# A two-layer graph transformer: the first norm ahead of the edge work, degrees in two halves, transposes in mid-chunk

## The chip, the cores and the metric

The kernel runs on one core of a Trainium2 chip. The metric is the device time of one execution in microseconds (us). The kernel before took 2141.93 us, the median of three runs (2136.43 to 2147.46 us).

## The reference, cut to what matters

There are 1250 nodes of 768 features and 20000 edges, sorted by destination. `src` and `dst` are lists of 20000 int32.

```python
xn = layernorm(x)
x = x + graph_attention(xn, src, dst) + linear_attention(xn)      # elu(q)+1, elu(k)+1, 12 heads
x = x + moe0(layernorm(x))                                        # 8 experts, top 2, one matrix each
xn = layernorm(x)
x = x + gcn_2_layers(xn, src, dst) + mix1(xn)                     # w_qkv, L2 norms over the nodes
x = x + moe1(layernorm(x))                                        # 8 experts, top 2, two matrices, gelu
# gcn: deg = segment_sum(ones, dst); dinv = rsqrt(deg); norm = dinv[src] * dinv[dst]
```

Everything is float32 in and out. The edges enter as a dense count matrix of 1250 x 1250, built on the chip from the two lists; the degrees are its sums (with one self loop for each node), and are used only in the second layer's GCN.

## The kernel before, in words

The nodes are cut into ten tiles of 125 rows (`NT`, `T`); X holds all of them in SBUF, XT holds the normalised rows transposed (six blocks of 128 features by 1250 nodes). Each engine has its own program, an instruction stream that runs in order, and the streams meet only at semaphores. TensorE's results go to eight PSUM banks in rotation: `plan_jobs` (L72) lists the jobs in order, job m uses bank m modulo 8, and `begin(m)` (L579) waits until the job eight places before has been emptied by the engine that owns it (`act` or `dve`). The consumer waits with `full(m)` for the count of filled jobs.

**Start.** SyncE (SP) issues the loads in this order (L412 to L463): the two edge lists EI, the first group of X (tiles 0 and 1), three small loads for the attention vectors (`wide`, `attn_sb`), the value weights of the first attention (`load(1)`), X's second group (tiles 2 to 5), its third (tiles 6 to 9), a bias, four small router loads (RWS, RBI), and WBD. ScalarE (ACT) issues the key weights first of all (L1055) on a queue of its own. VectorE (DVE) sets constants, then waits for the edge lists and does the edge work (L1324 to L1391): it casts the lists (EF), and in turns with TensorE (four jobs: `edges`, `spans`, `rng`, `attn_vec`) finds for each destination tile which edge tiles touch it, writes the table of turns, and places the attention vectors in vz. Only then come the first norms: `spread_of` (statistics), a square root by ACT (`root`), `normal` (writes XN).

**Key and value loop.** For each tile t, TensorE transposes tile t+1 (`transpose_tile`, L587) and multiplies tile t by the key and the value weights (`rows`, L605 through L645 and L646: 4 jobs of 6 matmuls, each of two passes in the profile). ACT copies the transposes to XT (`turned_tile`), takes the exponential of the keys and copies the values; DVE, which in iteration t first does statistics and norm of tile t+2, finishes the keys (L1436). On ACT `root(0, t+2)` stands at the head of iteration t, ahead of `turned_tile` and the exponentials of that iteration.

**Degrees and routing of the first expert layer.** After the graph attention TensorE sums the count matrix in 100 small matmuls (`deg`, L843 to L849, two columns each). They are issued between the router's logits and `route(1)`. On DVE `route` computes softmax and the top two (`sel_ready`), TensorE then forms the ranks (L857 to L859), DVE turns these to one-hot rows (`ranked`), TensorE makes the token lists (L864), DVE writes the table (`tab_ready`), and GpSimd (POOL) gathers the first expert's tokens.

**Second layer, q.** The 1250 columns are cut into five chunks of 250 (`QC`). For each chunk TensorE transposes the chunk's two tiles, waits until ACT has copied both to XT (L928), and computes six blocks of q (L932, 36 matmuls, 72 in the profile). Two copies by ACT empty each block (`q1_column`). Meanwhile DVE finishes the expert layer tile by tile: two weighted rows (`weighted`, from YG, gathered by POOL into four buffers), `normal` of the tile before, `spread_of` of this one. ACT's `root` of the next two tiles stand in the chunk, before columns 0 and 3 (L1229).

Of the kernel before, what the change touches and what calls it, by code (L numbers as in the profile page):

```python
# [9 lines left out]
ALU = mybir.AluOpType  # L10
ACT = mybir.ActivationFunctionType
# [60 lines left out]
def plan_jobs():  # L72
    j = Jobs()
    a, v = "act", "dve"
    j.add("edges", [v])
    j.add("spans", [v])
    j.add("rng", [v])
    j.add("attn_vec", [v])
    j.add("lnt0_0", [a] * 2)
    for t in range(NT):  # L80
        if t + 1 < NT:
            j.add(f"lnt0_{t + 1}", [a] * 2)
        j.add(f"kv{t}", [v, v, a, a])
    j.add("att_rows", [v] * 3)
# [43 lines left out]
def graph_transformer(nc, xn_d, y_d, x, src, dst, gW, gWT, gWresT, attnT, w0, wp0, bp0, rwT, rb, ewT, eb,  # L128
# [272 lines left out]
    def arrived(u):  # L401
# [6 lines left out]
        + [last(f"q1_{len(QC) - 1}", KC), last("k1", 18), last("v1", 18), last("proj1", 20), last("conv1", 20), last("conv2", 20)]  # L408

    @block.sync  # L410
    def _(sp):
        sp.dma_start(EI[:, 0:2, :], src.rearrange("(a p e) -> p a e", a=2, p=80)).then_inc(e_in, 16)  # L412
        sp.dma_start(EI[:, 2:4, :], dst.rearrange("(a p e) -> p a e", a=2, p=80)).then_inc(e_in, 16)
# [43 lines left out]
        for n, (w, b) in enumerate(((rwT, rb), (fgT, fbg))):  # L457
            sp.dma_start(RWS[:, n], w.rearrange("(k p) e -> p k e", p=P)).then_inc(small_in, 16)
            sp.dma_start(RBI[:, n], b.partition_broadcast(T)).then_inc(small_in, 16)
# [4 lines left out]
        for u in (2, 3):  # L464
            unit_left(u - 2)
            load(u)
        spare = 2 * N // P * P
# [22 lines left out]
        sp.wait_ge(pe_filled, J.filled(J.at["q1_0"]))  # L490
# [87 lines left out]
    def _(pe):  # L578
# [42 lines left out]
        pe.wait_ge(edge_f, 1)  # L621
        ps = begin(0)
        for k in range(4):
            last = nc.tensor.transpose(ps[0:T, k * 80:(k + 1) * 80], EF[:, k, :], ident[0:80, 0:80])
        last.then_inc(pe_filled, 1)
        pe.wait_ge(ranged, 1)
        ps = begin(J.at["spans"])
        for a in range(2):
            last = nc.tensor.transpose(ps[0:2 * NT, a * 80:(a + 1) * 80], hit[:, a, :, :].rearrange("p a b -> p (a b)"),
                                       ident[0:80, 0:80])  # L630
        last.then_inc(pe_filled, 1)
        pe.wait_ge(ranged, 2)
        ps = begin(J.at["rng"])
        nc.tensor.transpose(ps[0:1, 0:2 * NT], rng, ident[0:2 * NT, 0:2 * NT]).then_inc(pe_filled, 1)
        pe.wait_ge(gw_in, 48)
        ps = begin(J.at["attn_vec"])
        nc.tensor.matmul(ps[:, 0:2 * H], wide, attn_sb, start=True, stop=True).then_inc(pe_filled, 1)

        transpose_tile(0, 0, J.at["lnt0_0"])
        for t in range(NT):  # L640
            if t + 1 < NT:
                transpose_tile(0, t + 1, J.at[f"lnt0_{t + 1}"])
            pe.wait_ge(act_emptied, J.emptied("act", J.at[f"lnt0_{t}"] + 1))
            m = J.at[f"kv{t}"]
            rows(m, XT, weights(0), t)  # L645
            rows(m + 2, XT, weights(1), t)  # L646
        pe.wait_ge(vz_ready, 1)
# [196 lines left out]
        ps = begin(J.at["deg"])  # L844
        for t in range(NT):
            for s in range(NT):
                last = nc.tensor.matmul(ps[0:T, 2 * t:2 * t + 2], AT[:, s, t * T:(t + 1) * T], onesr[0:T, 0:2],
                                        start=(s == 0), stop=(s == NT - 1))
        last.then_inc(pe_filled, 1)  # L849

        def route(L):
# [8 lines left out]

            pe.wait_ge(ranked, k)
# [173 lines left out]
    def _(act):  # L1035
# [160 lines left out]
        ps = full(J.at["deg"])  # L1196
        nc.scalar.activation(DT, ps[0:T, 0:2 * NT:2], ACT.Sqrt).then_inc(deg_root, 1)
        nc.scalar.drain().then_inc(act_emptied, 1)
# [16 lines left out]
        def q1_column(c, q):  # L1215
            o, n = QC[c]
            ps = full(J.at[f"q1_{c}"] + q)
# [82 lines left out]
    def _(dve):  # L1300
# [23 lines left out]
        dve.wait_ge(e_in, 32)  # L1324
        V.tensor_copy(EF, EI).then_inc(edge_f, 1)

        ps = full(0)
        V.tensor_copy(ES.rearrange("p a b -> p (a b)"), ps[0:T, 0:320]).then_inc(dve_emptied, 1)
        for a in range(2):
            V.tensor_reduce(mnx[:, 0, a:a + 1], EF[:, 2 + a, :], AX.X, ALU.min)  # L1330
            V.tensor_reduce(mnx[:, 1, a:a + 1], EF[:, 2 + a, :], AX.X, ALU.max)
        V.drain()
        for a in range(2):
            V.tensor_scalar(hit[:, a, 0, :], gidx[:, 0, :], mnx[:, 1, a:a + 1], None, ALU.is_le)
        V.drain()
        for a in range(2):
            V.scalar_tensor_tensor(out=hit[:, a, 1, :], in0=gidx[:, 1, :], scalar=mnx[:, 0, a:a + 1],
                                   in1=hit[:, a, 0, :], op0=ALU.is_gt, op1=ALU.mult)
        V.drain()
        V.tensor_scalar(mnx[:, 0, :], tidx, -1.0, float(ET), ALU.mult, ALU.add)  # L1340
        V.tensor_scalar(mnx[:, 1, :], tidx, 1.0, None, ALU.add)
        V.drain()
        for a in range(2):
            V.tensor_scalar(hit[:, a, 0, :], hit[:, a, 1, :], mnx[:, 0, a:a + 1], None, ALU.mult)
        V.drain()
        for a in range(2):
            V.tensor_scalar(hit[:, a, 1, :], hit[:, a, 1, :], mnx[:, 1, a:a + 1], None, ALU.mult)
        V.drain().then_inc(ranged, 1)
        ps = full(J.at["spans"])
        V.tensor_reduce(rng, ps[0:2 * NT, 0:160], AX.X, ALU.max)  # L1350
        V.drain().then_inc(ranged, 1)
        V.drain().then_inc(dve_emptied, 1)
        ps = full(J.at["rng"])
        V.tensor_copy(span[:, 0:2, :].rearrange("p a b -> p (a b)"), ps[0:1, 0:2 * NT]).then_inc(dve_emptied, 1)
        V.drain()
        V.tensor_tensor(span[:, 3, :], span[:, 0, :], span[:, 1, :], ALU.add)
# [506 lines left out]
```

## Time and profile before

| | us |
|---|---|
| median of three runs | 2141.93 |
| the profiled execution, whole | 2141.64 |
| its span in the profile | 2139.8 |
| PE busy | 1928.0 (90%) |
| DVE busy | 757.1 (35%) |
| ACT busy | 397.3 (19%) |
| POOL busy | 132.0 (6%) |

The span runs from the first to the last instruction in the profile. PE is the matmul part of TensorE, PEld its weight loads, which overlap the matmuls. The order of time is: start to 27 us; key and value loop to 188; the rest of the first attention to 396; count matrix to 562; graph attention to 871; degrees and routing to 929; first experts to 1150; q, k and v of the second layer to 1420; projection and GCN to 1815; routing and second experts to the end. Stretches without matmuls lie at the start and around the two routings.

### The profile page before, as it was taken

How to read it: one execution, taken by the hardware profiler on the slowest of the kernel's cores; microseconds unless marked ns; L12 is line 12 of the kernel's file. 1: busy time of each engine (PE TensorE's matmuls, PEld its weight loads, DVE VectorE, ACT ScalarE, POOL GpSimd, SP SyncE). 2: the span in 40 equal slices, each digit the busy share in tenths (PEclk: the TensorE clock that was granted, in tenths of full speed). 3: DMA queues.
4: the chain of work that ended last, by engine and by line, in shares of the span. 5: the costliest groups of instructions: out<-in, count | busy, mean ns of one | idle time of the engine just before them, and what ended most of it. 6: DMA issues, size and time to landing. Idle time of an engine off the chain costs nothing.

```text
span 2139.8 us, 23079 instructions
## 1 busy us (share of the span) xinstructions
PE 1928.0 (90%) x7603; PEld 1234.0 (58%) x7604; DVE 757.1 (35%) x1715; ACT 397.3 (19%) x1046; POOL 132.0 (6%) x223
## 2 busy tenths in 40 slices
PE   5999999998999999779995999999999999399990
PEld 3555566566433446646663875555578589266560
DVE  3211322676688879411112511141111133311113
ACT  2331210024211112100100332000221211111110
POOL 0000000000000000011112300000000000111114
PEclk9999999999999999579997999999999999599995
DMA  6004000000000101424554410110010012434537
GB/s 174 0 1 155 2 0 1 19 1 0 20 29 28 42 21 44 162 74 176 188 180 131 139 59 0 44 45 0 0 45 1 0 59 61 159 125 170 183 118 223
DMA packets 58416, 154.05 MB, mean 72 GB/s; under 512 B 12574, under 2 KB 23218, under 8 KB 57893
## 3 DMA queue, kind: packets, MB, share of 16 engines
q1 hardware_dynamic: 34053, 87.05, 11.6%
q0 software_dynamic: 13200, 36.25, 5.5%
q10 hardware_dynamic: 11088, 29.77, 3.8%
q8 instruction: 46, 0.75, 0.1%
q14 instruction: 29, 0.24, 0.0%
HBM read 121.76 MB, written 34.78 MB: 73 GB/s over the span
## 4 chain that ended last, share of the span: by engine, by line
PE 86%; DMA 5%; DVE 4%; issue 2%; ACT 1%; DVEq 1%; POOL 1%; POOLq 0%; ACTq 0%; SPq 0%
PE PS L605 22%; PE PS L821 11%; PE PS L906 10%; PE PS L615 7%; PE PS L753 5%; PE PS L996 4%; PE PS L932 4%; PE PS L1016 4%; PE PS L669 4%; PE PS L973 3%; PE PS L959 3%; DMA WS<-in_fW 2%; DMA YG<-expert_rows,IDXA 2%; PE PS L884 1%; PE PS L803 1%
## 5 line engine op out<-in xcount | busy, mean ns | idle before, releaser
L605 PE MATMUL PS<-WS,XT 128*125 128x384 f32 x960 | 312.5, 487 | 1.4 <-issue 1.4
L821 PE MATMUL PS<-WR,F 125*65 125x500 f32 (+1 forms) x720 | 262.2, 518 | 2.5 <-DVE WR L1572 2.5
L605 PEld LDWEIGHTS PS<-WS,XT 128*125 128x125 f32 x960 | 180.0, 188 | 129.0 <-issue 2.6
L1572 DVE SCALAR_TENSOR_TENSOR WR<-RB,U,AT 125x500 f32<-125x500 f32 (+1 forms) x360 | 212.5, 647 | 22.0 <-PE PS L821 13.7
L906 PE MATMUL PS<-WS,XGT 128*128 x624 | 208.0, 490 | 0.0
L821 PEld LDWEIGHTS PS<-WR,F 125*65 125x65 f32 x720 | 97.6, 139 | 142.8 <-issue 99.8
L906 PEld LDWEIGHTS PS<-WS,XGT 128*128 128x128 f32 x624 | 117.7, 192 | 77.3 <-issue 2.5
L615 PE MATMUL PS<-XT,WS 128*128 128x416 f32 (+1 forms) x432 | 151.2, 512 | 0.0
L1698 DVE TENSOR_TENSOR YS<-PS,EBB 128x768 f32<-128x768 f32 x50 | 47.9, 958 | 270.5 <-PE PS L906 209.6
L615 PEld LDWEIGHTS PS<-XT,WS 128*128 128x128 f32 x432 | 81.6, 189 | 69.2 <-issue 69.2
L753 PE MATMUL PS<-OHS,OHD 125*125 125x418 bf16 x564 | 110.8, 351 | 0.0
L996 PE MATMUL PS<-WS,XGT 128*128 x300 | 103.9, 497 | 5.3 <-DMA WS<-in_fW 5.0
L1524 DVE TENSOR_SCALAR OHS<-iota,ES 125x1250 bf16<-125x1250 f16 x188 | 102.0, 543 | 0.0
L1016 PE MATMUL PS<-WS,HT 128*128 x288 | 96.8, 486 | 0.0
L1186 ACT ACTIVATE XGT<-PS 128x384 f32<-128x384 f32 x106 | 46.1, 489 | 256.0 <-DVE YS L1698 191.8
L753 PEld LDWEIGHTS PS<-OHS,OHD 125*125 125x125 bf16 x564 | 68.9, 137 | 39.3 <-DVE OHS L1524 23.8
L932 PE MATMUL PS<-XT,WS 128*128 128x250 f32 x360 | 78.9, 380 | 6.2 <-issue 6.2
L996 PEld LDWEIGHTS PS<-WS,XGT 128*128 128x128 f32 x300 | 56.3, 195 | 40.9 <-issue 8.6
L605 PE MATMUL PS<-WS,QT 128*125 128x384 f32 x240 | 78.9, 486 | 0.0
L932 PEld LDWEIGHTS PS<-XT,WS 128*128 128x128 f32 x360 | 68.8, 192 | 15.6 <-issue 7.4
L605 PE MATMUL PS<-WS,QK 128*125 128x384 f32 x240 | 77.6, 486 | 0.0
L1016 PEld LDWEIGHTS PS<-WS,HT 128*128 128x128 f32 x288 | 54.7, 190 | 38.2
(263 smaller groups left out, 1968.8 us busy)
## 6 DMA issues: line engine op xcount, KB each, us to landing
expert_rows<-YS ACTq DMA_DIRECT2D x50, 384.0 KB
WS<-in_ewT SPq DMA_DIRECT2D x8, 2304.0 KB, 10.6
WS<-in_fW SPq DMA_DIRECT2D x16, 1152.0 KB, 7.8
WS<-in_w SPq DMA_DIRECT2D x5, 2304.0 KB, 9.8
xn_rows<-XN ACTq DMA_DIRECT2D x20, 336.0 KB
RB<-expert_rows SPq DMA_DIRECT2D x12, 488.3 KB
WS<-in_wp SPq DMA_DIRECT2D x2, 2304.0 KB, 11.8
WS<-in_W SPq DMA_DIRECT2D x2, 2304.0 KB, 8.3
```

Of the source, the lines that this page charges most:

```text
L605: last = nc.tensor.matmul(ps[0:T, 0:HC], lhsT[:, k, t * T:(t + 1) * T], w[:, k, b * HC:(b + 1) * HC], start=(k == 0), stop=(k == KC - 1))
L615: last = nc.tensor.matmul(ps[:, 0:n], w[:, k, q * P:(q + 1) * P], rhs[:, k, o:o + n], start=(k == 0), stop=(k == KC - 1))
L669: last = nc.tensor.matmul(ps[:, 0:n], w[:, k, q * P:(q + 1) * P], XT[:, k, o:o + n], start=(k == 0), stop=(k == KC - 1))
L753: last = nc.tensor.matmul(PS[0:T, 3 * (g % 2) + c, 0:w], OHD[:, k, :], OHS[:, k, o:o + w], start=False, stop=True, skip_group_check=True)
L821: last = nc.tensor.matmul(PS[0:DW, 2 * (u % 2) + j, 0:n], F[:, s, 2 * p + j, :], WR[:, k % WSLOTS, j, 0:n], start=(s == 0), stop=(s == NT ...
L906: last = nc.tensor.matmul(PS[:, 4 + 2 * a + b, 0:HC], XGT[:, a, k, :], WS[:, bass.ds(slot, 1), k * C + b * HC:k * C + (b + 1) * HC].rearra ...
L932: last = nc.tensor.matmul(ps[:, 0:n], w[:, k, q * P:(q + 1) * P], XT[:, k, o:o + n], start=(k == 0), stop=(k == KC - 1))
L959: last = nc.tensor.matmul(ps[:, 0:n], HH[:, v, s, q * P:(q + 1) * P], AT[:, s, o:o + n], start=(s + v == 0), stop=(s == NT - 1 and v == 1))
L996: last = nc.tensor.matmul(PS[:, 2 + a, 0:FH], XGT[:, a, k, :], WS[:, bass.ds(slot, 1), k * FH:(k + 1) * FH].rearrange("p a b -> p (a b)"), ...
L1016: last = nc.tensor.matmul(PS[:, 5 + b, 0:HC], HT[:, k, :], WS[:, bass.ds(slot, 1), o:o + HC].rearrange("p a b -> p (a b)"), start=(k == 0) ...
L1524: V.tensor_scalar(OHS[:, k, :], iota[0:T, :], ES[:, 0, bass.ds(tile + k, 1)], None, ALU.is_equal).then_inc(oh_ready, 1)
L1572: V.scalar_tensor_tensor(out=WR[:, k % WSLOTS, j, 0:nt * T], in0=RBS[u % RSLOTS][:, j, 0:nt * T], scalar=U[:, s, h:h + 1], in1=AT[:, s, t0 ...
```

## The change

Three pieces of work are put elsewhere; no piece of the computation is added or taken away. (1) SP issues the first group of X before the edge lists and the value weights before the small loads; the router's loads go behind the weights of units 2 and 3. DVE goes from the constants to the first norms. The edge work is cut into four pieces, which DVE does in iterations 0 to 3 of the key and value loop, after the norm of tile t+2; TensorE does its jobs behind the matmuls of tiles 0, 1 and 2. (2) The degrees become two jobs of 50 matmuls, one before the ranks and one behind them; ACT takes two square roots. (3) Tiles 0 and 1 are transposed ahead of the first chunk of q, and each later pair in the middle of the chunk before its own, between blocks 2 and 3. ACT does both roots of the next pair at the head of the chunk and copies the pair between columns 2 and 3.

```diff
 def plan_jobs():
-    j.add("edges", [v])
-    j.add("spans", [v])
-    j.add("rng", [v])
-    j.add("attn_vec", [v])
...
         j.add(f"kv{t}", [v, v, a, a])
+        for name in {0: ["edges"], 1: ["spans"], 2: ["rng", "attn_vec"]}.get(t, []):
+            j.add(name, [v])
...
-                j.add("deg", [a])
+                j.add("deg0", [a])
             j.add(f"rank{L}", [v])
+            if L == 1:
+                j.add("deg1", [a])
             j.add(f"tokens{L}", [v])
         else:
+            for t in (0, 1):
+                j.add(f"lnt2_{t}", [a] * 2)
             for c in range(len(QC)):
-                j.add(f"lnt2_{2 * c}", [a] * 2)
-                j.add(f"lnt2_{2 * c + 1}", [a] * 2)
-                j.add(f"q1_{c}", [a] * KC)
+                j.add(f"q1a_{c}", [a] * 3)
+                for t in (2 * c + 2, 2 * c + 3):
+                    if t < NT:
+                        j.add(f"lnt2_{t}", [a] * 2)
+                j.add(f"q1b_{c}", [a] * 3)
...
     def _(sp):
-        sp.dma_start(EI[:, 0:2, :], src.rearrange("(a p e) -> p a e", a=2, p=80)).then_inc(e_in, 16)
-        sp.dma_start(EI[:, 2:4, :], dst.rearrange("(a p e) -> p a e", a=2, p=80)).then_inc(e_in, 16)
...
         x_group(0)
+        sp.dma_start(EI[:, 0:2, :], src.rearrange("(a p e) -> p a e", a=2, p=80)).then_inc(e_in, 16)
+        sp.dma_start(EI[:, 2:4, :], dst.rearrange("(a p e) -> p a e", a=2, p=80)).then_inc(e_in, 16)
+        load(1)
         sp.dma_start(wide[:, 0:D], gW).then_inc(gw_in, 16)
         sp.dma_start(wide[:, D:P], gW).then_inc(gw_in, 16)
         sp.dma_start(attn_sb, attnT).then_inc(gw_in, 16)
-        load(1)
         x_group(1)
         x_group(2)
...
-        for n, (w, b) in enumerate(((rwT, rb), (fgT, fbg))):      # moved behind load(2), load(3)
...
# TensorE: in the loop over t, behind rows(...) of tile t
+            if t == 0:
+                pe.wait_ge(edge_f, 1)
+                ps = begin(J.at["edges"])
+                for k in range(4):
+                    last = nc.tensor.transpose(ps[0:T, k * 80:(k + 1) * 80], EF[:, k, :], ident[0:80, 0:80])
+                last.then_inc(pe_filled, 1)
+            if t == 1:
+                pe.wait_ge(ranged, 1)
...
+            if t == 2:
+                pe.wait_ge(ranged, 2)
...
+                pe.wait_ge(gw_in, 48)
...
+        def degrees(half):
+            ps = begin(J.at[f"deg{half}"])
+            for i in range(5):
+                t = 5 * half + i
+                for s in range(NT):
+                    last = nc.tensor.matmul(ps[0:T, 2 * i:2 * i + 2], AT[:, s, t * T:(t + 1) * T], onesr[0:T, 0:2],
+                                            start=(s == 0), stop=(s == NT - 1))
+            last.then_inc(pe_filled, 1)
+
+        degrees(0)
...
             nc.tensor.matmul(ps[0:T, n:n + NE], ones[0:T, 0:T], SELB[:, NT, :], start=True, stop=True).then_inc(pe_filled, 1)
+            if L == 1:
+                degrees(1)
             pe.wait_ge(ranked, k)
...
+        for t in (0, 1):
+            transpose_tile(2, t, J.at[f"lnt2_{t}"])
+        w = weights(U_MIX1)
         for c, (o, n) in enumerate(QC):
-            for t in (2 * c, 2 * c + 1):
-                transpose_tile(2, t, J.at[f"lnt2_{t}"])
-            w = weights(U_MIX1)
             pe.wait_ge(act_emptied, J.emptied("act", J.at[f"lnt2_{2 * c + 1}"] + 1))
             for q in range(KC):
-                ps = begin(J.at[f"q1_{c}"] + q)
+                if q == 3 and c + 1 < len(QC):
+                    for t in (2 * c + 2, 2 * c + 3):
+                        transpose_tile(2, t, J.at[f"lnt2_{t}"])
+                ps = begin(J.at[f"q1a_{c}"] + q if q < 3 else J.at[f"q1b_{c}"] + q - 3)
...
# ScalarE
+        for half in range(2):
+            ps = full(J.at[f"deg{half}"])
+            nc.scalar.activation(DT[:, 5 * half:5 * half + 5], ps[0:T, 0:10:2], ACT.Sqrt).then_inc(deg_root, 1)
+            nc.scalar.drain().then_inc(act_emptied, 1)
...
         root(2, 0)
+        root(2, 1)
+        turned_tile(2, 0)
+        turned_tile(2, 1)
         for c in range(len(QC)):
-            turned_tile(2, 2 * c)
-            if c == 0:
-                root(2, 1)
-            turned_tile(2, 2 * c + 1)
+            for t in (2 * c + 2, 2 * c + 3):
+                if t < NT:
+                    root(2, t)
             for q in range(KC):
-                if q in (0, 3) and 2 * c + 2 + q // 3 < NT:
-                    root(2, 2 * c + 2 + q // 3)
+                if q == 3:
+                    for t in (2 * c + 2, 2 * c + 3):
+                        if t < NT:
+                            turned_tile(2, t)
                 q1_column(c, q)
...
# VectorE: in the loop over t, behind normal(0, t + 2) and ahead of the keys of tile t
+            if t == 0:
+                dve.wait_ge(e_in, 32)
+                V.tensor_copy(EF, EI).then_inc(edge_f, 1)
+            if t == 1:
+                ps = full(J.at["edges"])
...
+            if t == 2:
+                ps = full(J.at["spans"])
...
+            if t == 3:
+                ps = full(J.at["rng"])
...
-        dve.wait_ge(deg_root, 1)
+        dve.wait_ge(deg_root, 2)
```

## Rows read from the trace of the kernel before

**Rows 1.** The page: busy time of the engines; the chain that ended last.

```profile
PE 1928.0 (90%) x7603; PEld 1234.0 (58%) x7604; DVE 757.1 (35%) x1715; ACT 397.3 (19%) x1046; POOL 132.0 (6%) x223
...
PE 86%; DMA 5%; DVE 4%; issue 2%; ACT 1%; DVEq 1%; POOL 1%; POOLq 0%; ACTq 0%; SPq 0%
```

**Rows 2.** Timeline of the start (start us, us, engine, line, operation, idle before).

```profile
8.02 0.42 DVE L1325 CAST EF<-EI 80x500 f32<-80x500 int32 x1 [4.45 <-DMA EI<-in_dst]
...
8.58 1.10 PE L624 MATMUL PS<-ident,EF 80*125 80x80 f32 x4 [8.58 <-DVE EF L1325]
...
14.38 0.62 PE L637 MATMUL PS<-attn_sb,wide 64*128 64x24 f32 x2 [0.20 <-DMA attn_sb<-in_attnT]
...
20.22 1.02 DVE L1397 BATCH_NORM_STATS2 stats<-X 125x6 f32<-125x384 f32 x2
...
26.87 1.02 DVE L1397 BATCH_NORM_STATS2 stats<-X 125x6 f32<-125x384 f32 x2 [1.29 <-DMA X<-in_x]
26.94 16.64 PE L605 MATMUL PS<-WS,XT 128*125 128x384 f32 x48
...
28.91 0.68 DVE L1415 TENSOR_SCALAR XN<-X,mv,rstd 125x768 f32<-125x768 f32 x1
...
43.41 0.81 PE L592 MATMUL PS<-ident,XN 125*128 125x125 f32 x6
```

**Rows 3.** The tile WS to 60 us: key weights (L1055), value weights (L426).

```profile
L1055 ACTq DMA_DIRECT2D WS<-in_w x1: 507/507/507, 0.7 to 0.7; - x1
L426 SPq DMA_DIRECT2D WS<-in_w x1: 594/594/594, 4.9 to 4.9; - x1
...
DMA to landing us min/median/max: 13.0/14.0/15.0
```

**Rows 4.** Stretches of the start: busy by engine, clock, DMA share, GB/s.

```profile
4.00:5.00 1.00, 0.00 (x0) 0.00 (x0) 0.00 (x0) 0.00 (x0) 0.00 (x0) 1.00 1.03 413
...
10.00:11.00 1.00, 0.00 (x0) 0.00 (x0) 0.96 (x5) 0.00 (x0) 0.00 (x0) 1.00 1.08 320
...
0.00:20.00 20.00, 2.34 (x9) 1.61 (x10) 9.87 (x53) 1.28 (x1) 1.44 (x13) 1.00 0.94 303
```

**Rows 5.** Timeline of the degrees, the first routing and the first expert matmuls.

```profile
879.27 21.16 PE L847 MATMUL PS<-onesr,AT 125*125 125x2 f32 x100 [0.26 <-DVE LG L1556]
...
886.78 2.34 DVE L1638 TENSOR_TENSOR SELB<-SELB,SEL 125x8 f32<-125x8 f32 x10
...
901.74 0.24 DVE L1642 COPY RS<-PS 125x80 f32<-125x80 f32 x1 [12.62 <-PE PS L859]
...
912.55 1.18 PE L864 MATMUL PS<-TV,OHR 125*128 125x60 bf16 x20 [10.85 <-DVEq L1673]
...
928.71 6.47 PE L906 MATMUL PS<-WS,XGT 128*128 x12
```

**Rows 6.** Stretches at the end of the degrees, columns as in rows 4.

```profile
895.00:900.00 5.00, 5.00 (x25) 5.00 (x25) 0.00 (x0) 0.00 (x0) 0.00 (x0) 0.50 0.93 398
900.00:905.00 5.00, 1.70 (x9) 1.61 (x8) 2.47 (x14) 0.18 (x1) 0.00 (x0) 0.50 0.01 5
```

**Rows 7.** Timeline of TensorE: the second chunk of q to the third.

```profile
1198.92 15.42 PE L932 MATMUL PS<-XT,WS 128*128 128x250 f32 x72 [1.40 <-issue]
1214.18 1.45 PE L592 MATMUL PS<-ident,XN 125*128 125x125 f32 x12
1217.02 15.42 PE L932 MATMUL PS<-XT,WS 128*128 128x250 f32 x72 [1.39 <-issue]
```

**Rows 8.** Timeline of ACT and DVE there: root, weighted rows, copies to XT.

```profile
1207.72 0.20 ACT L1042 ACTIVATE std<-std 125x1 f32<-125x1 f32 x1
...
1210.43 2.12 DVE L1704 SCALAR_TENSOR_TENSOR X<-YG,GW,X 125x768 f32<-125x768 f32 x2
...
1215.31 1.61 ACT L1047 ACTIVATE XT<-PS 128x375 f32<-128x375 f32 x4
```

**Rows 9.** The tile YG in the stretch of q: the gathers' time to landing.

```profile
DMA to landing us min/median/max: 6.6/7.2/12.6
```

More of the change, by code:

```diff
@@ L619, in _ @@
         pe.wait_ge(consts, 1)
[L621 to L637, printed above, removed]
         transpose_tile(0, 0, J.at["lnt0_0"])
@@ L646, in _ @@
             rows(m + 2, XT, weights(1), t)
+            if t == 0:
[6 more added lines that the diff above has]
+                pe.wait_ge(ranged, 1)
+                ps = begin(J.at["spans"])
+                for k in range(2):
+                    last = nc.tensor.transpose(ps[0:2 * NT, k * 80:(k + 1) * 80],
+                                               hit[:, k, :, :].rearrange("p a b -> p (a b)"), ident[0:80, 0:80])
+                last.then_inc(pe_filled, 1)
+            if t == 2:
+                pe.wait_ge(ranged, 2)
+                ps = begin(J.at["rng"])
+                nc.tensor.transpose(ps[0:1, 0:2 * NT], rng, ident[0:2 * NT, 0:2 * NT]).then_inc(pe_filled, 1)
+                pe.wait_ge(gw_in, 48)
+                ps = begin(J.at["attn_vec"])
+                nc.tensor.matmul(ps[:, 0:2 * H], wide, attn_sb, start=True, stop=True).then_inc(pe_filled, 1)
         pe.wait_ge(vz_ready, 1)
@@ L843, in _ @@
         pe.wait_ge(loops, NT)
[L844 to L849, printed above, removed]
+        def degrees(half):
[5 more added lines that the diff above has]
+                                            start=(s == 0), stop=(s == NT - 1))
+            last.then_inc(pe_filled, 1)
+        degrees(0)
         def route(L):
@@ L1335, in _ @@
[L1335 to L1354, printed above, removed]
@@ L1377, in _ @@
-        V.drain()
-        V.tensor_copy(table, span[:, 2:5, :])
-        V.drain().then_inc(table_ready, 1)
-        ps = full(J.at["attn_vec"])
-        V.tensor_copy(vv, ps[:, 0:2 * H]).then_inc(dve_emptied, 1)
-        V.drain()
-        vzf = vz.rearrange("p a b -> p (a b)")
-        step = AR + 2
-        for side in range(2):
-            for r in range(2):
-                o = side * 32 + r
-                V.tensor_copy(vzf[r * D:(r + 1) * D, o:o + 5 * step + 1:step],
-                              vv[r * D:(r + 1) * D, side * H + r:side * H + r + H - 1:2])
@@ new lines, in _ @@
+            if t == 2:
+                ps = full(J.at["spans"])
+                V.tensor_reduce(rng, ps[0:2 * NT, 0:160], AX.X, ALU.max)
+                V.drain().then_inc(ranged, 1)
+                V.drain().then_inc(dve_emptied, 1)
+            if t == 3:
+                ps = full(J.at["rng"])
+                V.tensor_copy(span[:, 0:2, :].rearrange("p a b -> p (a b)"), ps[0:1, 0:2 * NT]).then_inc(dve_emptied, 1)
+                V.drain()
+                V.tensor_tensor(span[:, 3, :], span[:, 0, :], span[:, 1, :], ALU.add)
+                V.tensor_scalar(span[:, 2, :], span[:, 0, :], -1.0, float(ET), ALU.mult, ALU.add)
+                V.drain()
+                V.tensor_scalar(span[:, 3, :], span[:, 3, :], float(-ET), 1.0, ALU.add, ALU.max)
+                V.drain()
+                V.tensor_scalar(span[:, 7, :], span[:, 3, :], 1.0 / SLOTS, None, ALU.mult)
+                V.drain()
+                V.tensor_tensor(turns, span[:, 7, :].unsqueeze(2).to_broadcast([1, NT, ET // SLOTS]),
+                                io128[0:1, 0:ET // SLOTS].unsqueeze(1).to_broadcast([1, NT, ET // SLOTS]), ALU.is_gt)
+                V.drain()
+                V.tensor_reduce(span[:, 3, :], turns, AX.X, ALU.add)
+                V.drain()
+                V.tensor_scalar(span[:, 6, :], span[:, 3, :], float(-SLOTS), float(ET), ALU.mult, ALU.add)
+                V.memset(span[:, 5, :], 0.0)
+                V.drain()
+                V.tensor_tensor(span[:, 2, :], span[:, 2, :], span[:, 6, :], ALU.min)
+                V.tensor_tensor_scan(out=span[:, 4, :], data0=span[:, 3, :], data1=span[:, 5, :], initial=0.0, op0=ALU.add, op1=ALU.add)
+                V.drain()
+                V.tensor_tensor(span[:, 4, :], span[:, 4, :], span[:, 3, :], ALU.subtract)
+                V.drain()
+                V.tensor_copy(table, span[:, 2:5, :])
+                V.drain().then_inc(table_ready, 1)
+                ps = full(J.at["attn_vec"])
+                V.tensor_copy(vv, ps[:, 0:2 * H]).then_inc(dve_emptied, 1)
+                V.drain()
+                vzf = vz.rearrange("p a b -> p (a b)")
+                step = AR + 2
+                for side in range(2):
+                    for r in range(2):
+                        o = side * 32 + r
+                        V.tensor_copy(vzf[r * D:(r + 1) * D, o:o + 5 * step + 1:step],
+                                      vv[r * D:(r + 1) * D, side * H + r:side * H + r + H - 1:2])
+                V.drain().then_inc(vz_ready, 1)
```

66 lines of the change are left out of this document (27 added, 39 removed).

## The prediction

> **What bounds the kernel now.** I read the page first: PE is busy for 90% of the span and holds 86% of the chain that ended last, the other engines far less [rows 1]. The reader should see from this that only two things can move the time: work taken from PE, and stretches in which PE stands still. This change takes no work from PE, so I looked for the stillness with the timeline, in three places. At the start the first key matmul runs at 26.94 us [rows 2]. The degrees keep PE busy for 21.16 us, and in that time the routing's next step waits: DVE sits idle 12.62 us before L1642 [rows 5]. Between two chunks of q PE stands for 1.39 or 1.40 us, four times in all [rows 7].
>
> **Step 1, the start.** Before, DVE begins the first statistics at 20.22 us, after all edge work, and the first key matmul follows 6.72 us later (26.94 - 20.22): two norms, two sets of transposes, the copy to XT [rows 2]. X's first group was there by then, since DVE did not wait for it. After the change the first statistics wait only for X's first group. Its landing before isn't shown. It is 2 tiles x 125 rows x 3072 B = 0.77 MB. The queues move 413 GB/s at best, and 320 when SP's and ACT's transfers run side by side [rows 4]. Bounds: from a start of data at about 2 us, alone it needs 1.9 us, so 4.3 with the end of the transfer; at the top, the attention vectors, queued behind X on SP, had landed by 14.4 us [rows 2]; X now goes out 0.9 us earlier and with the lists behind it, so I set 12.5 (an estimate). I take half of 320 GB/s, 4.8 us, so 7.6 us with 0.8 for start and end, since the key weights flow beside it all the time. That puts the first key matmul at 7.6 + 6.7 = 14.3 us at the earliest.
>
> It also needs the key weights. They were issued at 0.7 and landed 13.0 us later, at 13.7 [rows 3]. Less than that is unlikely, more is likely: X now competes from the first byte, where before the lists did. If both queues moved equal bytes until the 2.36 MB of key weights had landed, 4.72 MB would have to pass at the 303 GB/s of the first 20 us [rows 4]: 15.6 us, plus 1.7 before data flows, 17.3 us. I take 14.8, nearer to the row of before, because SP's queue has the edge lists in rows of 500 B behind X, and in that stretch it moves few bytes. So the first key matmul goes from 26.94 to 14.8: 12.1 us gained.
>
> The Trainium skill, page "DMA: Bandwidth & Descriptors", section "Queues, rings and completion order", says that each DMA engine takes turns between the queues that have work, packet by packet. The rate falls from 413 to 320 GB/s when the second queue has work [rows 4], which agrees with taking turns but does not show equal bytes. By equal turns in bytes the time is the 17.3 us above, which I keep as a rival.
>
> The value weights are needed 7.7 us after the first key matmul (half of 16.64 us less the cold start [rows 2]), at 22.5. They landed at 4.9 + 15.0 = 19.9 [rows 3] and have three small loads less ahead: no wait. X's second group made DVE wait until 26.87 [rows 2]; what stands ahead of it in SP's queue is the same in sum, so I keep 26.9. Its norm was written 2.72 us later (28.91 + 0.68 - 26.87), so at 29.6. DVE then casts the lists, 0.42 us [rows 2]: 30.1. PE leaves tile 0 at 14.8 + 16.5 = 31.3 and asks for the cast first and for the transposes of tile 2 next: 1.2 us of slack, and this is the wait that is late next. Behind this DVE wait stand the keys of tile 0 and behind ACT's root its exponentials and value copies; PE asks for these banks only in tile 1's third and later jobs, after 35 us, so nobody waits for them.
>
> PE takes over what it did in idle time before: 4 transposes in 1.10 us, the attention vectors' two in 0.62 [rows 2], three more small ones for spans and rng at about 0.2 each, 2.35 us at the top. These were at the pace of a PE that had been idle, 0.275 us a transpose; in the loop six take 0.81, 0.135 each [rows 2]. So about half: 1.3 us. DVE's pieces (0.42, about 3.4, 0.4 and 4.8 us in iterations 0 to 3) lie beside 16 us of matmuls per tile. The one for tile t is ready some 10 us before PE asks, because ACT's root, which holds it up, runs about 2 us after the tile before is done. If that cover were gone the price would be 9 us once. SP's later router loads stand ahead of the first use by hundreds of microseconds. Step 1: 12.1 - 1.3 = 10.8 us; bounds 5.5 (X at 12.5) and 12.5 (weights at 13.7, takeover at 0.7).
>
> **Step 2, the degrees.** 100 matmuls in 21.16 us are 0.212 us each [rows 5], at a granted clock of 0.50, the 1.2 GHz level [rows 6]. After the change the first 50 take 10.58 us and end at 889.85. The selection was ready at 886.78 + 2.34 = 889.12 [rows 5], so the ranks start 10.58 us earlier, and DVE's L1642 at 891.2. DVE needs 912.55 - 901.74 = 10.8 us from there to the token matmuls [rows 5]: 902.0. PE does the second half from 891.1 to 901.7. It is hidden with 0.3 us to spare, which is thin: every microsecond that it took longer would be lost one to one. The gain is bounded above by the selection, 900.43 - 889.2 = 11.2. Below, if the second half started late or ran 1 us longer, 9.5. Step 2: 10.6 us. Downstream, the expert weights, issued at the same event as before, have landed by 900 (398 GB/s, then 5 [rows 6]), and their first use moves from 928.7 [rows 5] to 918.1. ACT's second root needs a few tenths beside the 1.18 us of the token matmuls.
>
> **Step 3, q.** Four waits of 1.39 or 1.40 us [rows 7] are ACT's copies to XT; the 12 transposes stay on PE (1.45 us a pair [rows 7]). In mid-chunk nobody waits for the copies: three blocks, 7.7 us, lie behind. Gain 4 x 1.4 = 5.6 us. What is late next is the second tile's norm. ACT ends the last column of a chunk, and is free for the next root, 1.1 us after PE has left it (1215.31 - 1214.18 [rows 7, 8]). From a root to the weighted rows, with the norm and the next tile's statistics between, are 2.7 us (1210.43 - 1207.72), the weighted rows take 2.12 [rows 8], and the second norm's reciprocal and its 0.68 [rows 2] some 0.9: 6.8 us. PE asks after three blocks, half of 15.42 [rows 7], 7.7 us. Slack 0.9 us. The first chunk begins as before and is longer. Gathers must be there too: the weighted rows in the middle need the pair that was issued nearly a chunk (16.7 us) before, against 7.2 us median and 12.6 us longest to landing [rows 9]. Bounds: 0 (a stall of 1.4 us in each chunk) and 5.6.
>
> **Sum.** 10.8 + 10.6 + 5.6 = 27.0 us. The profiled execution took 2141.64 us, 1.84 above its span of 2139.8, and would become 2114.6 (span 2112.8). It stands 0.3 us under the median, so I predict 2115.
>
> **The rivals.**
> A. *The start is bound by transfers.* Key weights at 17.3 or X's first group at 12.5 (first matmul at 17.3 to 19.2). For it: the DMA share is full from 2 us on [rows 4]. Against: the same bytes passed before. Gain 2.5 to 4.4 less: 2118 to 2119.
> B. *A new wait in mid-chunk.* The slack of 0.9 us is my sum of parts; with 1 us more in each chunk beyond it the pairs stall PE by 1 us, with 2.4 more step 3 is undone: 2119 to 2124. With A, 2128. For it: a weighted row stands inside the chain. Against: DVE is otherwise idle.
> C. *Given back.* PE comes earlier to something paced by a transfer, and 15 us or more are lost there: 2130 to 2141. The expert weights speak against it, landed 18 us ahead of use.
> D. *Slower: the gathers pace the chunks.* XN of the second tile stands behind the weighted rows of the tile after, so a late gather holds PE in mid-chunk where before it had the rest of the chunk. Each gather would have to land in some 28 us instead of 7.2 [rows 9], at 12 us more in each of four chunks: 48 - 27 = 21 us slower, 2163. It decides from 6.8 us of stall a chunk on.
> E. *The change doesn't do what it says:* the degrees' second half is not hidden, because the ranks free DVE later than PE; then step 2 gives 0 to 5 us: 2120 to 2125. The 0.3 us of margin speak for a little of it, not for all.
>
> **How the numbers follow.** Forecast 0.60 (own range 2110 to 2120, from the bounds of the steps); A 0.14; B 0.12; E 0.05; C 0.05; D 0.04. The runs of before lie 11 us apart, so 4 us are added at either end. The range of 2106 to 2128 leaves out C, D and a little at each end. About 0.5% (10.7 us) can be told from no change here: faster (below 2131) 0.90, same 0.06, slower 0.04.
>
> **What would show it.** Right: the first key matmul near 14.8 and the second tile's near 32.5; token matmuls near 902.0 less the 10.8 of step 1; L932's groups of 36 with the transposes between them and no idle time after; degrees as 50 and 50. Wrong: PE idle before L592 in mid-chunk (B), a DMA as what ended the wait before the first key matmul beyond 15.5 us (A), PE busy with degrees when `ranked` comes (E), or one of the later stretches longer than before (C).

## The result and the profile after

The changed kernel takes 2120.61 us (median of 4 runs, 2116.09 to 2123.16), the kernel before on the same chip 2140.18 (4 runs, 2136.43 to 2147.46): a ratio of 0.9892, 95% interval 0.9859 to 0.9925. Faster, by 19.6 us; 27.0 were forecast. The profiled execution took 2120.68 us, its span 2118.9.

The page, to be read against [rows 1]: busy time, then TensorE's granted clock in 40 slices.

```profile
PE 1932.0 (91%) x7603; PEld 1238.7 (58%) x7604; DVE 756.5 (36%) x1715; ACT 397.0 (19%) x1047; POOL 131.9 (6%) x223
...
PEclk9999999999899999689997999999999999599995
```

PE does the same 7603 matmuls, yet it is busy 4.0 us longer than before. The instructions didn't change, so some of them ran at a lower clock.

The start, as [rows 2] (start us, us, engine, line, operation, idle before):

```profile
8.35 1.02 DVE L1350 BATCH_NORM_STATS2 stats<-X 125x6 f32<-125x384 f32 x2 [3.84 <-DMA X<-in_x]
...
15.06 17.03 PE L609 MATMUL PS<-WS,XT 128*125 128x384 f32 x48
...
27.08 1.02 DVE L1350 BATCH_NORM_STATS2 stats<-X 125x6 f32<-125x384 f32 x2 [13.38 <-DMA X<-in_x]
...
29.72 0.41 DVE L1387 CAST EF<-EI 80x500 f32<-80x500 int32 x1
...
31.93 0.56 PE L637 MATMUL PS<-ident,EF 80*125 80x80 f32 x4
...
32.33 0.81 PE L596 MATMUL PS<-ident,XN 125*128 125x125 f32 x6
...
32.97 15.65 PE L609 MATMUL PS<-WS,XT 128*125 128x384 f32 x48
```

The transfers into the tile WS, as [rows 3]:

```profile
L1071 ACTq DMA_DIRECT2D WS<-in_w x1: 502/502/502, 0.7 to 0.7; - x1
L428 SPq DMA_DIRECT2D WS<-in_w x1: 449/449/449, 2.8 to 2.8; - x1
...
DMA to landing us min/median/max: 14.1/15.4/16.8
```

DVE now waits for X alone (8.35), and the key weights land at 0.7 + 14.1 = 14.8. The four edge transposes cost PE 0.56 us, half of [rows 2].

The degrees and the routing, as [rows 5]:

```profile
875.07 10.66 PE L856 MATMUL PS<-onesr,AT 125*125 125x2 f32 x50 [0.26 <-DVE LG L1580]
...
885.59 0.69 PE L868 MATMUL PS<-SEL,before 125*125 125x80 f32 x2
...
886.85 10.64 PE L856 MATMUL PS<-onesr,AT 125*125 125x2 f32 x50
...
897.85 1.18 PE L877 MATMUL PS<-TV,OHR 125*128 125x60 bf16 x20 [0.36 <-DVEq L1697]
...
913.87 8.83 PE L919 MATMUL PS<-WS,XGT 128*128 x24
```

The ranks stand between two halves, and the token matmuls follow the second half after 0.36 us.

The chunks of q, as [rows 7]:

```profile
1174.38 15.35 PE L948 MATMUL PS<-XT,WS 128*128 128x250 f32 x72
1189.57 1.45 PE L596 MATMUL PS<-ident,XN 125*128 125x125 f32 x12
1190.85 15.35 PE L948 MATMUL PS<-XT,WS 128*128 128x250 f32 x72
```

No row here has an idle bracket any more. The groups of 72 are two halves of neighbouring chunks, with the transposes in mid-chunk.

One stage grew, and the forecast had no term for it: the count matrix, from its first one-hot matmul to the first attention matmul. Before, then after (stretch, its length; busy time of PE, weight loads, DVE, ACT, POOL; granted clock, DMA share, GB/s):

```profile
401.30:562.40 161.10, 143.24 (x811) 98.58 (x811) 116.79 (x371) 53.06 (x178) 0.00 (x0) 0.99 0.01 4
```

```profile
389.20:558.30 169.10, 151.42 (x811) 106.15 (x810) 117.02 (x372) 52.69 (x176) 0.00 (x0) 0.93 0.01 4
```

The same 811 matmuls take 8.2 us more of PE at a mean clock of 0.93 instead of 0.99. Each stage, taken between the same two instructions in both traces:

| stage | before | after | difference | forecast |
|---|---|---|---|---|
| to the first key matmul | 26.94 | 15.06 | -11.9 | -12.1 |
| keys and values (takeover) | 161.1 | 162.6 | +1.5 | +1.3 |
| to the count matrix | 213.3 | 211.5 | -1.7 | 0 |
| count matrix | 161.1 | 169.1 | **+8.0** | 0 |
| graph attention to the degrees | 316.9 | 316.8 | -0.1 | 0 |
| degrees to the first expert matmul | 49.4 | 38.8 | -10.6 | -10.6 |
| experts to q | 250.4 | 248.9 | -1.5 | 0 |
| q | 89.4 | 83.8 | -5.6 | -5.6 |
| the rest | 871.3 | 872.3 | +1.0 | 0 |
| sum | | | -20.9 | -27.0 |

Two of the smaller differences can be read too. The -1.7 us is a stretch of 3.4 us at the lower clock level at 295 us, which the profile before has and the one after lacks. The experts' -1.5 us lies in the scatter: the changed kernel's profiles have 248.9 to 250.0 there.

So the question was what the 8.0 us are: the change's doing (for example because the earlier start puts the stage at another place in time), or the execution's.

### The profile page after: what moved, and what is told of

Read it like the earlier page. It is cut to its first block, busy times and chain, and to the rows that moved or that the text cites. A ratio compares the mean times of both kernels' runs of the same rounds, so it can differ in the third digit from the quotient of the medians.

```text
span 2118.9 us, 23084 instructions
## 1 busy us (share of the span) xinstructions
PE 1932.0 (91%) x7603; PEld 1238.7 (58%) x7604; DVE 756.5 (36%) x1715; ACT 397.0 (19%) x1047; POOL 131.9 (6%) x223
## 4 chain that ended last, share of the span: by engine, by line
PE 86%; DMA 5%; DVE 4%; issue 2%; ACT 1%; DVEq 1%; POOL 1%; POOLq 0%; ACTq 0%; SPq 0%
PE PS L609 22%; PE PS L827 11%; PE PS L919 10%; PE PS L619 7%; PE PS L759 5%; PE PS L1012 4%; PE PS L948 4%; PE PS L1032 4%; PE PS L675 4%; PE PS L989 3%; PE PS L975 3%; DMA WS<-in_fW 2%; DMA YG<-expert_rows,IDXA 2%; PE PS L897 1%; PE PS L809 1%
## 5 line engine op out<-in xcount | busy, mean ns | idle before, releaser
L619 PE MATMUL PS<-XT,WS 128*128 128x416 f32 (+1 forms) x432 | 151.2, 512 | 0.0
L619 PEld LDWEIGHTS PS<-XT,WS 128*128 128x128 f32 x432 | 81.6, 189 | 69.2 <-issue 69.2
L759 PEld LDWEIGHTS PS<-OHS,OHD 125*125 125x125 bf16 x564 | 71.6, 141 | 39.7 <-DVE OHS L1548 22.8
L675 PE MATMUL PS<-XT,WS 128*128 128x416 f32 (+1 forms) x216 | 76.1, 513 | 0.0
## 6 DMA issues: line engine op xcount, KB each, us to landing
WS<-in_ewT SPq DMA_DIRECT2D x8, 2304.0 KB, 10.6
```

The lines of the kernel that those rows point to most:

```text
L619: last = nc.tensor.matmul(ps[:, 0:n], w[:, k, q * P:(q + 1) * P], rhs[:, k, o:o + n], start=(k == 0), stop=(k == KC - 1))
L675: last = nc.tensor.matmul(ps[:, 0:n], w[:, k, q * P:(q + 1) * P], XT[:, k, o:o + n], start=(k == 0), stop=(k == KC - 1))
L759: last = nc.tensor.matmul(PS[0:T, 3 * (g % 2) + c, 0:w], OHD[:, k, :], OHS[:, k, o:o + w], start=False, stop=True, skip_group_check=True)
```

## The experiments

**The parts one by one.** Each of three kernels is the one before with one part of the change.

```
# e1: X's first group ahead of the lists, first norm first, edge jobs in tiles 0 to 2
+        for name in {0: ["edges"], 1: ["spans"], 2: ["rng", "attn_vec"]}.get(t, []):
+            j.add(name, [v])
...
# e2: the degrees in halves around the ranks
+        degrees(0)
...
+                degrees(1)
...
# e3: the next pair's transposes in mid-chunk
+                j.add(f"q1a_{c}", [a] * 3)
...
+                j.add(f"q1b_{c}", [a] * 3)
```

> Only part 1 of the change: first norm ahead of the edge work, edge work in the key and value loop, SP's new order; degrees and q as before. Theory S (each part's gain adds up and is real, and what is missing from the sum was lost to dips of the granted clock in the count matrix): the first key matmul near 15.1 us, the stage behind the key and value loop (first attention row matmuls) near 177.7 instead of 188.05, so 10.4 us gained there, and the whole time 10 us below before, give or take the clock dips (0.9 us each). Rival G (what the start gains is given back in the count matrix because that stage starts at another time): the count matrix stage takes 168 to 169 us instead of 161 here too, and the whole time is only 2 to 3 us below before.

> Only part 2: degrees in halves around the ranks. Nothing ahead of the count matrix changes. Theory S: from the first degree matmul to the first expert matmul 38.8 us instead of 49.4, whole time 10.6 us below before. Rival R (random dips of the clock from execution to execution): the same in the median, but the count matrix stage of this profile, whose instructions are the same and begin at the same time as before, has another number of dips than before's one. Rival G says it takes 161 us as before.

> Only part 3: transposes of the next pair in mid-chunk. Theory S: the chunks of q take 84 us instead of 89.5, no wait ahead of a chunk, whole time 5.6 us below before (0.26%). Rival B of the prediction (a new wait in mid-chunk) would show idle time ahead of the transposes: it should be none.

Measured, 12 runs each, against 29 runs of the kernel before (median 2144.31): the start alone 2133.76 (ratio 0.9945, 0.9927 to 0.9963), the degrees alone 2135.93 (0.996, 0.9941 to 0.9979), q alone 2138.65 (0.998, 0.9963 to 0.9997). These are 10.6, 8.4 and 5.7 us; the steps were 10.8, 10.6 and 5.6. In the traces the three places behave as in the whole change. The first key matmul of e1:

```profile
14.85 17.62 PE L603 MATMUL PS<-WS,XT 128*125 128x384 f32 x48
```

The degrees of e2, 38.5 us from the first degree matmul to the first expert matmul, against 49.4:

```profile
883.28 10.66 PE L852 MATMUL PS<-onesr,AT 125*125 125x2 f32 x50 [0.26 <-DVE LG L1566]
...
921.78 9.54 PE L915 MATMUL PS<-WS,XGT 128*128 x24
```

And q of e3 takes 84.0 us, without idle time ahead of the transposes. The count matrix stage of the three, e1, e2 and e3 in this order:

```profile
389.20:554.00 164.80, 146.90 (x811) 102.37 (x810) 117.27 (x373) 52.58 (x176) 0.00 (x0) 0.96 0.01 4
```

```profile
401.80:569.30 167.50, 149.75 (x810) 104.85 (x809) 116.95 (x372) 52.66 (x176) 0.00 (x0) 0.95 0.01 4
```

```profile
402.30:571.40 169.10, 151.33 (x811) 106.14 (x810) 116.92 (x371) 52.66 (x176) 0.00 (x0) 0.93 0.01 4
```

This decides a good deal. In e2 and e3 nothing has been changed ahead of this stage; it begins within 1.0 us of where it began before, and it takes 6.4 and 8.0 us longer than in the execution of before. The long stage needs no part of the change.

**The changed kernel again.** No edit, in three further comparisons.

> The changed kernel once more. Theory R (dips of the clock fall at random from one execution to the next): another number of dips in the count matrix, between 1 and 8, and a time that moves by 0.9 us for each; median 2114 to 2121. Theory G (they belong to the moved start): again about 8 dips, the stage again 168 to 169 us, the median again near 2120.6.

> The changed kernel a third time, for comparison on the same chip. Theory R: again another number of dips (0 to 8), the count matrix stage 159.3 us plus 1.6 us for each; median between 2108 and 2121.

> The changed kernel a fourth time on the same chip as e9. Theory R: runs from 2106 up to 2123, scatter several times that of e9, median 2 to 8 us above e9. Rival: no difference in median or scatter.

Measured: 2110.36 (5 runs, ratio 0.9847, 0.9821 to 0.9872), 2117.1 (6 runs, 0.9859, 0.9828 to 0.989), 2115.98 (6 runs, 0.9879, 0.9852 to 0.9906). The stage in the profiled executions of e4 and e10:

```profile
391.60:550.90 159.30, 141.67 (x811) 97.24 (x809) 116.55 (x371) 53.05 (x178) 0.00 (x0) 1.00 0.01 4
```

```profile
389.20:555.10 165.90, 148.27 (x811) 103.14 (x809) 116.33 (x371) 52.81 (x177) 0.00 (x0) 0.96 0.01 4
```

The same kernel, 159.3 and 165.9 us, with 169.1 in the first profile; e6 had 159.3 as well, at a clock of 1.00. Where the time goes is seen in short stretches of the first profile after, around 475 us:

```profile
472.00:475.60 3.60, 1.99 (x12) 1.73 (x13) 1.71 (x6) 1.57 (x4) 0.00 (x0) 0.95 0.00 0
475.60:479.00 3.40, 3.40 (x14) 2.70 (x14) 0.71 (x2) 2.68 (x12) 0.00 (x0) 0.55 0.00 0
479.00:482.50 3.50, 3.50 (x22) 2.67 (x21) 3.48 (x12) 0.00 (x0) 0.00 (x0) 1.00 0.00 0
```

PE is busy for all of the middle stretch, but gets 14 matmuls done where the next one has 22: the granted clock is at its lower level (1.2 GHz) for nearly all of it, and then back. Just ahead of it lies the end of a group of the count matrix:

```profile
470.68 1.11 PE L739 MATMUL PS<-ident,AROW 125*125 125x125 f32 x8
472.76 0.48 PE L739 MATMUL PS<-ident,AROW 125*125 125x125 f32 x2 [0.96 <-ACT AT L1126]
474.10 0.74 PE L751 MATMUL PS<-zeros 125*125 125x418 bf16 x3 [0.85 <-issue]
474.67 2.21 PE L733 MATMUL PS<-WBD,XT 128*125 128x128 f32 x12
```

PE stands still twice there, 0.96 and 0.85 us. There are nine such ends between the ten groups, and a low stretch follows some of them. I counted these in each profile: 0 in e4 and e6 (159.3 us), 1 before (161.1), 3 in e1 (164.8), 4 in e10 (165.9), 5 in e2 (167.5), 6 in e3 and in the first profile after (169.1). That is 159.3 us plus 1.6 to 1.8 for each. The times of whole executions follow: 2120.68 with six, 2110.84 (e6) with none. That they are 9.8 us apart, just what the stage is (169.1 - 159.3), is partly luck. The first profile after also has a low stretch of 6.8 us at 557 us, right behind the stage. It makes the graph attention 316.8 us instead of e6's 314.0, and other stages are shorter by as much. The profile of before has such a stretch too (at 561 us, 316.9 us), so this one cancels in the table above.

The number is not drawn afresh at each group end. The profiles of the later kernels below belong here too: without a fill, e7 had 0, and e8, e11 and e12 had 6 each. Of the eight profiles with the changed start and no fill whose edge lists stand behind X, the stage began at 391.2 to 391.8 us in e4, e6 and e7, and these had none. It began at 389.2 to 389.5 in the other five (first after, e1, e8, e10, e11), and these had 3 to 6. The three later ones had a low stretch at 285 us, which the five lacked. So what happened earlier in the execution goes with the number. It is no rule by itself: before, e2 and e3 all had that early stretch, at 295 to 297 us, and then 1, 5 and 6. The Trainium skill, page "TensorE: Matmul & The Clock Gate", section "What's actually happening", says of the slow matmuls at a kernel's start that their number differs from run to run of the same kernel; these rows show the same in the middle of one.

**Filling the gaps.** To the changed kernel ten matmuls of zeros are added at each group end, five behind each of the two rounds of transposes at which PE stands.

```
+        def fill(g):
+            for i in range(5):
+                nc.tensor.matmul(PS[0:T, 3 * ((g + 1) % 2) + i % 3, 0:416], zeros[:, 0:T], zeros[:, 0:416], start=True, stop=True)
...
+                    if q:
+                        fill(g)
```

> The changed kernel, with ten more matmuls of zeros (125x416, bf16, 0.17 us each at the 2.4 GHz level) in each of the nine group ends of the count matrix, where TensorE waits twice for about 1 us (0.96 and 0.97). They write zeros to banks that are zeroed again afterwards. Theory R (the dips of the granted clock to 1.2 GHz, 3.4 us long and 1.6 us of time each, come where TensorE stands still at the group ends, and how many of them occur differs from execution to execution): hardly a dip left in the count matrix, the stage at 160 us (at most 2 us more where the zeros don't fit in the waits), median near 2110 with less scatter. Rival (the dips have nothing to do with the waits): the number of dips as in other executions, the stage 1 to 10 us longer than 160.

> The kernel of e5_fill again (zero matmuls in the waits of the count matrix). Theory R: all runs again in a narrow band near 2110 (2106 to 2113), no dip in the count matrix, stage 160.5 us. Rival (the narrow band of e5 was luck): runs up to 2120 as the changed kernel has them.

Measured: 2111.18 (5 runs, 2107.12 to 2111.79; ratio 0.9828, 0.9801 to 0.9855) beside 2117.1 for the changed kernel on the same chip, and 2111.21 (5 runs, 2109.56 to 2113.68; 0.9855, 0.9826 to 0.9883) beside 2115.98. The stage of e5, then of e9:

```profile
391.70:552.10 160.40, 157.02 (x902) 107.62 (x900) 116.58 (x371) 52.90 (x177) 0.00 (x0) 1.00 0.01 4
```

```profile
389.30:549.60 160.30, 157.06 (x902) 107.67 (x900) 116.41 (x371) 52.78 (x176) 0.00 (x0) 1.00 0.01 4
```

A group end of e5:

```profile
456.88 1.12 PE L739 MATMUL PS<-ident,AROW 125*125 125x125 f32 x8
457.83 1.04 PE L747 MATMUL PS<-zeros 125*125 125x416 bf16 x5
458.96 0.48 PE L739 MATMUL PS<-ident,AROW 125*125 125x125 f32 x2
459.28 1.04 PE L747 MATMUL PS<-zeros 125*125 125x416 bf16 x5
```

PE no longer stands here; of the stops at the group ends one is left in this profile, 0.83 us behind the first group. The stage costs 1.0 to 1.1 us more than the 159.3 of an undisturbed one, and had no low stretch in either profile. The two profiles don't weigh the same. In e5 the stage began at 391.7 us, where the changed kernel had no low stretch either. In e9 it began at 389.3, where all five profiles without the fill had 3 to 6: this is the one that speaks for the fill. The ten runs lie between 2107.12 and 2113.68, where the 21 of the changed kernel lie between 2106.16 and 2123.16. But the five runs of e4, without a fill, are as narrow (2107.92 to 2112.63), so only the comparisons on the same chip count: 2106.16 to 2122.45 beside e5, 2112.28 to 2120.96 beside e9. It is the best version found, 5.9 us (e5) and 4.8 us (e9) under the changed kernel in the medians. The intervals of the ratios overlap, so the size is less sure than the direction. Between the two stops PE does transposes; whether they have a part in the low stretches beside the stops, no run tests.

**X in smaller groups.**

```
-XGROUPS = [(0, 2), (2, 6), (6, 10)]
+XGROUPS = [(0, 1), (1, 2), (2, 6), (6, 10)]
```

> The changed kernel with X's first group cut in two, so that the first norm waits for tile 0 alone. Theory X (the first key matmul is bound by X's landing at 8.35 us plus 6.7 us): statistics begin 1.5 to 2.5 us earlier. Theory W (the key weights, landed at 14.8, bind as well): the first key matmul moves by 0.3 us at most, from 15.1 to 14.8, and the whole time does not change measurably.

Measured: 2117.38 (4 runs, ratio 0.9866), beside 2117.1 for the changed kernel.

```profile
6.55 1.02 DVE L1351 BATCH_NORM_STATS2 stats<-X 125x6 f32<-125x384 f32 x2 [2.05 <-DMA X<-in_x]
...
10.62 1.02 DVE L1351 BATCH_NORM_STATS2 stats<-X 125x6 f32<-125x384 f32 x2 [1.34 <-DMA X<-in_x]
...
14.71 5.72 PE L610 MATMUL PS<-WS,XT 128*125 128x384 f32 x11
```

Tile 0's statistics begin 1.8 us earlier, tile 1's now wait for their own transfer, and PE's order has tile 1's transposes ahead of tile 0's keys: 0.35 us came of it at the first key matmul. The key weights landed at 13.2 here and were not what it waited for.

**Edge lists ahead of X**, the rest as changed.

```
-        x_group(0)
         sp.dma_start(EI[:, 0:2, :], ...)
         sp.dma_start(EI[:, 2:4, :], ...)
+        x_group(0)
```

> The changed kernel with the edge lists ahead of X in SP's queue again, nothing else. If SP's order made part of the gain: X lands near 12.5 us instead of 8.35, the first key matmul near 19 instead of 15, 4 us lost. If only DVE's order counted: X near 9.5 us, first key matmul near 16.

Measured: 2122.75 (1 run).

```profile
13.61 1.02 DVE L1350 BATCH_NORM_STATS2 stats<-X 125x6 f32<-125x384 f32 x2 [9.11 <-DMA X<-in_x]
...
20.34 16.95 PE L609 MATMUL PS<-WS,XT 128*125 128x384 f32 x48
```

The first matmul comes 20.34 - 13.61 = 6.73 us after X, as 15.06 - 8.35 = 6.71 after the change. So X's landing sets the start, and its place ahead of the lists is worth 5.3 us of step 1. The time of the whole execution is a single run, whose stage of the count matrix had six low stretches, so no difference is read from it; the same holds for e8 and e11 below.

**The degrees split 40 and 60.**

```
-            for i in range(5):
-                t = 5 * half + i
+            for i in range((4, 6)[half]):
+                t = 4 * half + i
```

> The changed kernel with the degrees split 40 and 60 matmuls instead of 50 and 50. The theory that the second half is hidden behind DVE's 10.8 us with a few tenths to spare: the ranks start 0.7 us earlier (the selection is then what they wait for) and the token matmuls wait for TensorE: from the first degree matmul to the token matmuls 24.2 us instead of 22.8. Rival (there is slack of 2 us or more): 22.1 us.

Measured: 2116.39 (1 run).

```profile
872.99 8.56 PE L856 MATMUL PS<-onesr,AT 125*125 125x2 f32 x40 [0.26 <-DVE LG L1580]
...
882.96 0.71 PE L868 MATMUL PS<-SEL,before 125*125 125x80 f32 x2 [1.41 <-DVEq L1663]
...
884.24 12.74 PE L856 MATMUL PS<-onesr,AT 125*125 125x2 f32 x60
...
896.85 1.18 PE L877 MATMUL PS<-TV,OHR 125*128 125x60 bf16 x20
```

PE waits 1.41 us for the selection, then the longer second part ends last: 23.9 us from the first degree matmul to the tokens, against 22.8. The second part is what ends last ahead of the token matmuls here. But that is no loss yet, since the next step is DVE's, which takes the tokens (L1713). With 50 and 50 DVE comes to it from a table of its own:

```profile
900.14 0.20 DVE L1711 CAST TAB<-XT 1x90 int32<-1x90 f32 x1
900.42 0.19 DVE L1713 TENSOR_SCALAR TOKF<-PS 128x30 f32<-128x30 f32 x1
```

The token matmuls had ended at 899.03 (897.85 + 1.18), 1.4 us before. With 40 and 60:

```profile
898.07 0.19 DVE L1713 TENSOR_SCALAR TOKF<-PS 128x30 f32<-128x30 f32 x1 [0.33 <-PE PS L877]
```

DVE waited 0.33 us for PE, and the ranks had begun 0.5 us earlier (10.9 us after the first degree matmul, against 11.4). The first expert matmul came at 911.43, 38.4 us after the first degree matmul, against 38.8, and 38.5 to 38.9 in all ten profiles with 50 and 50. So the 40 and 60 lost nothing by the end of the stage; one run can't tell it from the 50 and 50.

**The transposes one block earlier.**

```
-                if q == 3 and c + 1 < len(QC):
+                if q == 2 and c + 1 < len(QC):
```

> The changed kernel with the next pair's transposes after two blocks of a chunk instead of three (ACT's copies likewise). The prediction's chain from a chunk's start to the second tile's norm takes 7.4 us in the changed kernel's trace (1189.12 against a chunk at 1181.97), so with PE there at 5.1 us it should wait some 2.2 us in the three later chunks, and the chunks of q take 88 to 91 us instead of 83.8. Rival (that chain has more room than the sum says): no wait, 84 us.

Measured: 2121.18 (1 run), q 85.5 us against 83.8.

```profile
1184.56 0.81 PE L596 MATMUL PS<-ident,XN 125*128 125x125 f32 x6
...
1186.69 0.86 PE L596 MATMUL PS<-ident,XN 125*128 125x125 f32 x6 [1.33 <-DVE XN L1368]
...
1204.35 0.86 PE L596 MATMUL PS<-ident,XN 125*128 125x125 f32 x6 [0.97 <-DVE XN L1368]
```

The second tile's norm is what is late next, as step 3 had named it, but in two chunks only and by less than was expected. The reason is that PE does the six transposes of the first tile before it needs the second norm, and the expectation counted from the first. In the changed kernel's trace PE comes to the second tile at 1190.21, 1206.68 and 1223.15, and the norms had been written at 1189.12, 1205.22 and 1220.02: slacks of 1.1, 1.5 and 3.1 us. One block earlier (2.56 us), that gives waits of 1.5, 1.1 and none; 1.33, 0.97 and none were measured.

## Why the prediction held

**Step 1** was forecast at 10.8 us; the first key matmul and the takeover give 11.9 - 1.5 = 10.4, and the part alone 10.6. The key weights landed at 14.8, as forecast. X landed at 8.35 and not at 7.6, and this decides: 8.35 + 6.71 is the 15.06 of the first matmul. The forecast had weights as the later of the two. e7 and e12 show that it was X's path. A split of the queues by equal bytes (weights at 17.3, rival A) did not come. The transfers of this trace, counted by queue, show why. From 8 to 10 us both queues moved 203 packets, but ACT's were of 3072 B and SP's of 463 B in the mean (lists and small loads): 312 and 47 GB/s. From 11 to 13 us both had packets of 3 KB and moved 203 GB/s each. So the turns were equal in packets, and the forecast's reason for 14.8, few bytes in SP's rows of 500 B, is what happened. The slack ahead of the cast was larger than the 1.2 us of the forecast: it was written at 30.13, and PE began the edge transposes at 31.93. The takeover is less sure than 1.5 against 1.3 looks. The first key matmuls ran slower (17.03 us for 48, before 16.64), and e2 and e3, whose start is that of before, took 162.1 and 162.0 us for this stage where before took 161.0.

**Step 2** gave 10.6 us, as forecast. Its margin to the token matmuls was as thin as forecast: the second half ends at 897.49, the token matmuls start 0.36 us later, and in e8, where the second part ends 1.6 us later, they start 1.1 us later. But the forecast took the token matmuls for the end of the path ("every microsecond that it took longer would be lost one to one"), and that is not borne out. Their result lay ready for 1.4 us before DVE took it, so the real margin was some 1.7 us (an estimate, 0.36 and what e8 leaves of the 1.4), and e8's first expert matmul came no later. Rival E did not come. The part alone measured 8.4 us, and its interval (4.5 to 12.7 us, the ratio's times 2144.31) holds 10.6.

**Step 3** gave 5.6 us, and 5.7 alone, though the interval of that one is wide (0.6 to 7.9 us). The chain to the second norm was longer than the forecast's: it was written at 1189.12, 0.45 us before PE had done its three blocks (1189.57), against 0.9. What the forecast left out is that PE transposes the first tile before the second, 0.64 us, so the smallest slack was 1.1 us, and e11 bears that out. Rivals B and D did not come.

**The sum** was right in its mechanism: the three places gave 10.4 + 10.6 + 5.6 = 26.6 us in the traces, and 24.6 us as the sum of the parts alone. The first comparison alone would not have shown it. The four comparisons of the changed kernel with the one before gave 19.6, 33.9, 28.3 and 24.8 us, 26.7 in the mean, and the 21 runs of the changed kernel have a median of 2115.98 against the 2115 forecast. That the agreement is this close is luck, since the runs lie 17 us apart and the comparisons 14. The difference in the first comparison looked like rival C, time given back, and the sign that the forecast had named for it, a later stretch longer than before, was there. It isn't: the stage that grew has no waits that others don't have, and executions without the change have it too. What the forecast lacked was a term for this spread, up to 9.8 us in one stage between two executions of the same kernel; its range had 4 us at either end for the scatter of whole runs. The profile of before was one at the short end in this stage (161.1 us, 159.3 being the shortest seen), and its 2141.64 us are 2.7 under the median of 29 runs, 2144.31, though 0.3 from the median of the three that were shown. What decides how many low stretches an execution gets stays open; the fill shows only that with PE kept at work over the group ends they were not seen, in two profiles.

## What to carry to other kernels

Set a sum against a profile stage by stage, between the same instructions, and look at the granted clock of each stage before a difference is given a cause: the same kernel's stage took 159.3 and 169.1 us. An order of work that removes idle time is worth just the idle time if what is late next has slack. Work out that slack up to the instruction that really waits: at the degrees it was 0.4 us to the token matmuls but some 1.7 to DVE's use of them, and in q it was 0.45 us to the pair but 1.1 to the second tile. When a stage repeats short stops of PE, a few matmuls of zeros in them can cost less than the clock that is lost after them: here 1.0 to 1.1 us against up to 9.8.

## What the hardware did that I had not expected

Back-to-back matmuls did not raise the clock in the degrees: 50 of them with two columns each take 10.66 us at a granted clock of 0.50, and so did 100 in 21.16 us before [rows 5, 6]. The stretch after, around them, with PE busy for 33.24 of 46 us:

```profile
869.00:915.00 46.00, 33.24 (x167) 31.78 (x166) 19.14 (x89) 5.85 (x11) 4.50 (x10) 0.50 0.52 197
```

And 160 KB of lists (80 x 500 x 4 B) in rows of 500 B, put ahead of X in its queue, delay X by 5.3 us (13.61 - 8.35), as much as some 1.7 MB would at the 320 GB/s of [rows 4] (an estimate). X is issued 0.9 us later for it (1.65 against 0.73); the rest is in the transfers. From 3 to 5 us SP's queue began one packet in that run, while ACT's moved 350 GB/s; why it stood still, no run shows.
